# Later turns of the normalised input in the feed-forward stage of a transformer block, one core

## What is computed

```
x  = x + attention(layernorm(x))            # its last product, with Wo, is done in the last stage
h  = layer_norm(layernorm(x), ln1_g, ln1_b)
h  = gelu(h @ ternary(w1).T + b1)
h  = layer_norm(h, ln2_g, ln2_b)
x  = x + h @ ternary(w2).T + b2
```

## Time and profile before

| | |
|---|---|
| median of 3 runs | 3494.17 us (3492.02 to 3497.58) |
| the profiled execution | 3496.95 us, its span 3495.2 us, granted clock 0.989 |
| PE busy over the span | 3416.4 us (98%) |
| DVE / ACT / POOL busy | 75% / 66% / 75% |
| last stage | from about 2956 us to the end |

### The profile page before, as it was taken

One profiled execution on the slowest core, in us unless ns is written; L12 is line 12 of the kernel. 1 busy time (PEld: TensorE's weight loads), 2 busy tenths in 40 slices (PEclk: granted clock), 3 DMA queues, 4 the chain that ended last, 5 costly groups with the idle time before them and its releaser, 6 DMA issues. The chain is left out here.

```text
span 3495.2 us, 71907 instructions
## 1 busy us (share of the span) xinstructions
PE 3416.4 (98%) x21410; PEld 2203.3 (63%) x21410; DVE 2627.8 (75%) x4493; ACT 2297.5 (66%) x4412; POOL 2605.8 (75%) x1279
## 2 busy tenths in 40 slices
PE   6999999999999999999999999999999998999999
PEld 4655555555555555555555555666666654888888
DVE  6777777777777767777777777777777776899998
ACT  2766666776667667766667667776666665555555
POOL 2888888888888888888888888888888884222221
PEclk7999999999999999999999999999999998999999
DMA  5233322233333322333333323333322223333332
GB/s 195 83 95 105 107 95 99 94 122 101 101 101 122 101 83 99 118 101 101 101 118 100 101 96 119 101 101 101 119 92 92 74 84 103 94 98 92 98 99 67
DMA packets 255090, 355.75 MB, mean 102 GB/s; under 512 B 40221, under 2 KB 163485, under 8 KB 250269
## 3 DMA queue, kind: packets, MB, share of 16 engines
q1 hardware_dynamic: 245532, 343.29, 30.3%
q10 hardware_dynamic: 9216, 8.39, 0.7%
HBM read 219.49 MB, written 62.12 MB: 81 GB/s over the span
## 5 line engine op out<-in xcount | busy, mean ns | idle before, releaser
L463 POOL TENSOR_TENSOR prob_sum<-prob_sum,prob 128x1024 f32<-128x1024 f32 x762 | 1861.6, 2443 | 369.0 <-ACT prob L542 318.1
L542 ACT ACTIVATE prob<-scores 128x512 f32<-128x512 f32 x2048 | 1073.3, 600 | 524.2 <-PE scores L828 512.2
L752 DVE TENSOR_REDUCE row_max<-max_scores 128x1 f32<-128x512 f32 x1536 | 988.1, 684 | 435.0 <-PE max_scores L870 417.6
L1033 PE MATMUL attn_out<-prob,v 128*64 128x512 f32 x4096 | 934.9, 598 | 0.0
L819 PE MATMUL scores<-q_hi,k_hi 64*128 64x512 f32 x2048 | 786.7, 416 | 11.6 <-ACT prob L542 7.9
L824 PE MATMUL scores<-q_hi,k_lo 64*128 64x512 f32 x2048 | 755.7, 395 | 0.0
L828 PE MATMUL scores<-q_lo,k_hi 64*128 64x512 f32 x2048 | 752.1, 393 | 0.0
L1033 PEld LDWEIGHTS attn_out<-prob,v 128*64 128x64 f32 x4096 | 277.6, 137 | 566.6 <-issue 542.9
L870 PE MATMUL max_scores<-k_hi,q_hi 64*128 64x512 f32 x1536 | 579.2, 431 | 8.1 <-DVE row_max L752 5.0
L513 ACT ACTIVATE scores<-neg_max_seeds 128x512 f32<-128x512 f32 x1024 | 552.7, 599 | 48.8 <-DMA neg_max_seeds<-neg_max_halves 48.5
L819 PEld LDWEIGHTS scores<-q_hi,k_hi 64*128 64x128 f32 x2048 | 376.8, 185 | 290.1 <-issue 122.8
(11 more groups left out here) (148 smaller groups left out, 4771.6 us busy)
## 6 DMA issues: line engine op xcount, KB each, us to landing
rows<-rows SPq DMA_DIRECT2D x512, 128.0 KB, 2.0
neg_max_seeds<-neg_max_halves SPq DMA_DIRECT2D x128, 512.0 KB, 3.9
w_group<-w_parts SPq DMA_DIRECT2D x30, 1536.0 KB, 8.6
attn_normalised<-z_stage SPq DMA_DIRECT2D x128, 256.0 KB, 2.1
v<-attn_normalised SPq DMA_DIRECT2D x64, 512.0 KB, 4.1
sum_inverted_rows<-sums_inverted SPq DMA_DIRECT2D x126, 256.0 KB, 4.0
x_turned_parts<-x_tile_parts SPq DMA_DIRECT2D x49, 256.0 KB, 2.8
xt_batch<-x_turned_parts SPq DMA_DIRECT2D x7, 1792.0 KB, 9.3
```

The costliest lines, as they stand in the source:

```text
L463: nc.gpsimd.tensor_tensor(sums_of(k, half), a, prob[:, n % RING, :, :], ALU.add).then_inc(added, 1)
L542: nc.scalar.activation(prob[:, n % RING, e, :], S[e][n % 2][:, :], ACT.Exp).then_inc(exped[e], 1)
L752: nc.vector.reduce_max(mx[1 - u][:, e, n // 2, n % 2:n % 2 + 1], bank_of(e, jj)[:, :], axis=AX.X)\
L1033: nc.tensor.matmul(O[rows(e), :], V[k // 2 % 2][:, j, col:col + DH], prob[:, n % RING, e, :], start=j == 0, stop=j == 7).then_inc(pv_made[ ...
```

## The change

Three blocks of the last stage move inside the step functions; no instruction is added or dropped, and no wait condition is changed. On PE the two transposes `turn_b` go from between UP and `turn_c` to the end of the step, behind the down product. On ACT `h_turned_hi` goes from ahead of `g_turned_hi` to behind the gelu. On DVE `h_turned_lo` goes from the end of the step that turned the tile into the next step, between the gained gelu and `result`; it is thereby put under the phase UP.

```diff
@@ scalar
-                if at(j, q, Y_MADE):
-                    t, r = at(j, q, Y_MADE)
-                    wait(act, b_turned, t + 1)
-                    wait(act, up_made, 2 * t)
-                    nc.scalar.activation(hthi[:, :], TB[:, 0:KT * P], ACT.Copy).then_inc(ht_hi, 1)
                 if at(j, q, GATE):
...
                     nc.scalar.activation(gel[r % 2][:, :], up[:, :], ACT.Gelu, accum_out=gsum[r % 2][:, :]).then_inc(gelu_made, 1)
+                if at(j, q, Y_MADE):
+                    t, r = at(j, q, Y_MADE)
+                    wait(act, b_turned, t + 1)
+                    wait(act, up_made, 2 * t)
+                    nc.scalar.activation(hthi[:, :], TB[:, 0:KT * P], ACT.Copy).then_inc(ht_hi, 1)
                 if at(j, q, RES):
@@ vector
                                                    ALU.add, ALU.mult).then_inc(gained, 1)
+                if at(j, q, UP):
+                    t, r = at(j, q, UP)
+                    wait(dve, ht_hi, t + 1)
+                    wait(dve, up_made, 2 * t)
+                    nc.vector.tensor_tensor(htlo[:, :], TB[:, 0:KT * P], hthi[:, :], ALU.subtract).then_inc(ht_lo, 1)
                 if at(j, q, RES):
...
-                if at(j, q, Y_MADE):
-                    t, r = at(j, q, Y_MADE)
-                    wait(dve, ht_hi, t + 1)
-                    wait(dve, up_made, 2 * t)
-                    nc.vector.tensor_tensor(htlo[:, :], TB[:, 0:KT * P], hthi[:, :], ALU.subtract).then_inc(ht_lo, 1)
             steps(step)(dve)
@@ tensor
                         last.then_inc(up_made, 1)
-                if at(j, q, Y_MADE):
-                    t, r = at(j, q, Y_MADE)
-                    wait(pe, xg_made, t + 1)
-                    wait(pe, ht_lo, t)
-                    for k in range(KT):
-                        last = nc.tensor.transpose(TB[:, k * P:(k + 1) * P], xg[:, k * P:(k + 1) * P], ident[:, :])
-                    last.then_inc(b_turned, 1)
                 if at(j, q, GATE):
...
                     last.then_inc(down_made, 1)
+                if at(j, q, Y_MADE):
+                    t, r = at(j, q, Y_MADE)
+                    wait(pe, xg_made, t + 1)
+                    wait(pe, ht_lo, t)
+                    for k in range(KT):
+                        last = nc.tensor.transpose(TB[:, k * P:(k + 1) * P], xg[:, k * P:(k + 1) * P], ident[:, :])
+                    last.then_inc(b_turned, 1)
             steps(step)(pe)
```

## The result

| | before | after |
|---|---|---|
| median of 4 runs each | 3493.72 us | 3469.35 us (3466.45 to 3472.96) |
| ratio, 95% interval | | 0.9928 (0.9915 to 0.9940) |
| the profiled execution, its span | 3496.95, 3495.2 us | 3466.45, 3464.6 us |
| a step in the loop, mean of 56 | 8.164 us | 7.743 us |

What follows compares the result with a forecast made beforehand. A round over PE and DVE, `turn_b` waiting for `x_gained`, was taken as the bound; 19.3 us from loop steps, 0.5 from written-out steps and 0.3 from fill and drain gave 20.1 us, so 3474.1 us, range 3466 to 3485.

Steps and rivals of the forecast that it cites:

- What bounds, and why it goes: Loop of the last stage: a closed round over PE and DVE, `turn_b` waiting for `x_gained`, sets the 8.17 us step.
- PE's step: PE in the loop: 8.16 - 0.62 + 0.28 = 7.82 us per step, bounds 7.74 and 7.90.
- The removed part: PE between UP and `turn_c`: 2.48 us falls to 1.86, so 0.62 us go from a loop step.
- The part put in: `turn_b` behind the down product: 0.20 us from start to start, plus 0.08 on the first eight matmuls of Y.
- The gelu round: Negated mean, `h_turned_lo`, `up_biased`, gelu, next negated mean: 7.77 us, 0.05 under PE's step, bounds 7.69 and 7.91.
- DVE's list: DVE's same instructions, one of them moved, need 7.66 us per step, less than PE's 7.82.
- The rival in which this round takes over: Loop: the gelu round binds at 7.91 to 8.0 us per step, gain 9 to 14 us, 3480 to 3485; 22%.
- The delay at a turn of the loop: Register work a loop turn adds to DVE and ACT, hidden behind PE before, comes to light; part of the 22% rival.
- ACT's walk: ACT after Y's start: `h_turned_hi` from 0.3 us, `zn_hi` from 1.0 to 1.2, DVE's `zn_lo` about 2.1; no cost to PE.
- DVE alone: Loop: PE's step falls under DVE's, gelu round binds at 7.69 to 7.77 us; gain 23 to 27.5 us, 3467 to 3471; 15%.
- Fill and drain: Ends of the last stage: drain +1.7 us, fill about -2.0, together -0.3, bounds -2.5 and +1.7.
- the wait named: Drain, step 66: UP waits for `h_turned_lo` behind the gained gelu, +1.7 us.

Runs made afterwards that it cites:

- turn_constant: Kernel before, in its old order, but `turn_b` turns a constant tile (the bias rows) and PE does not wait for `x_gained`: 3462.55 us, one run.
- low_part_twice: Changed kernel, but DVE makes the low part of `turn_b` twice, first into a tile nobody reads: 3484.68 us.

## Why the prediction was right, and where it was off

The forecast was 3474.1, the measured 3469.35, within the range 3466 to 3485; faster, as forecast.

**What bounds, and why it goes: right.** `turn_constant` shows it without any move: take the wait away and the step is 7.74. The view that gave this was the chain, closed over PE and DVE; the waits view alone would have promised 0.19 or 0.63 per step, by the row that one takes, where 0.41 came.

**PE's step, 7.82 forecast, 7.75 measured: a term mis-sized.** The removed part was right: UP to `turn_c` is 1.87 after, 1.86 in the earlier trace rows. The part put in was 0.20 + 0.08; measured is 0.14 + 0.08 = 0.22 behind the down product, and 0.22 again in the old place without its wait. The row for the 0.20 was from a step in which `turn_b` had itself waited for `x_gained`, so its weight load lay bare; where nothing is awaited that load starts ahead, beside the down product. The weight loads of the two, in the fill of before and in the loop after (the transposes start at 2972.24 and at 3347.08):

```profile
2972.24 0.20 PEld L1307 LDWEIGHTS turn_b<-ident,x_gained 128*128 128x128 f32 x2 [0.39 <-DVE x_gained L1258]
...
3346.98 0.24 PEld L1325 LDWEIGHTS turn_b<-ident,x_gained 128*128 128x128 f32 x2
```

The old step's 0.27 to `turn_c` carried the same excess. This is 0.06 of the 0.07 per step, and most of the 4 us between the loop's forecast 19.3 and its 23.6.

**The gelu round, 7.77 forecast, 7.58 measured: too high by three small things.** The terms of the recorded sum add up to 7.78. `h_turned_lo` has a pitch of 0.33, not 0.41; the step from `up_biased` to the gelu costs 0.03, not 0.12 (1.43 from start to start); and the negated mean follows by 1.18. Durations of neighbours overlap by 0.06 to 0.1, and I had used them where pitches were to be had. The same goes for DVE's list: 7.66 forecast, 7.53 measured. The conclusion "0.05 under PE's" was thereby too near: it is 0.17. The rival in which this round takes over, given 22%, was further off than I thought, and `low_part_twice` shows that it starts at about 0.17 us more for DVE. The delay at a turn of the loop, which I feared there, does appear: the first two steps of a turn take 7.86 and 8.0 by DVE's starts. That it is the register work, and not the branch, was assumed and not tested. DVE makes it good with steps of 7.58 behind them, and PE, with 1.1 us of cover, never sees it.

**ACT's walk: right**, to 0.1 us: `h_turned_hi` 0.36 behind Y (0.3), `zn_hi` 1.06 (1.0 to 1.2), `zn_lo` 2.15 (2.1). The strict order of ACT's queue that the Trainium skill states (TensorE: Matmul & The Clock Gate, Architectural detail) agrees with it: `zn_hi` does not pass `h_turned_hi`, which waits 0.43 us for `turn_b`.

**The case "DVE alone" did not occur**, though its band of times (3467 to 3471) holds the result. PE binds at 7.75: with 0.24 us less for PE the step falls, with DVE alone as the bound it could not. Y still takes 0.120 per matmul with nothing awaited. By the formula of that page of the Trainium skill (Back-to-back issue gap), which the page gives for isolated matmuls, it would be 0.109, and no run here shows that.

**Fill and drain.** The drain cost 1.9 (1.7 forecast), by the wait named. The fill gave 3.1 (2.0 forecast), in three parts. The first, 0.9, is the granted clock ahead of UP of step 3, which no term of the prediction held and the change did not cause. The second, 0.8, lies between that UP and the first gained gelu (4.72 us instead of 5.53): ahead of the first gelu ACT loads a table, 1.28 us, and that load stood behind the wait of `h_turned_hi`, where now it comes during it. This the prediction had left out. The third, 1.4, lies from there to step 6: `turn_c` no longer waits behind `turn_b` in step 4 and runs at the 2.4 GHz level, where before PE had sat idle for 2.48 us and then had a mean granted clock of 0.54 from 2979.91 to 2983.60. The rows of before stand ahead of those of after:

```profile
2973.12 1.28 ACT L1198 ACT_TABLE_LOAD   x1
...
2980.35 1.91 PE L1316 MATMUL turn_c<-ident,gelu_gained 128*128 128x128 f32 x8
...
2963.02 1.28 ACT L1193 ACT_TABLE_LOAD   x1
...
2972.71 1.03 PE L1309 MATMUL turn_c<-ident,gelu_gained 128*128 128x128 f32 x8
```

What the order and what the clock gave in this third part was not separated. PE's move alone (`pe_only`) gained 1.3 us in the fill: 0.5 by the clock in the first part, nothing in the second (5.54 us), 0.8 in the third. Without the clock's 0.9, fill and drain come to the -0.3 us of the forecast, though by parts that it had not all named.

## What to carry to other kernels

When two busy engines wait for each other in a ring, look for a small consumer that stands directly behind a short cover and could run a few microseconds later; here that cost nothing once its consumers had moved along on every engine. A part of the move is a gamble: PE's part alone gave 20 us, PE's and ACT's without DVE's cost 69 (`pe_and_act`: +2%). Price the insertion by a row in which the operation waited for nothing, and use starts, not durations, for rounds. An order with room (2 us for `x_gained`) has a shorter mean step than a tighter one with the same sum when an engine is delayed now and then, as at the turns of this loop: 7.743 against 7.798. The times could not show it, for the drain gave most of it back. Before a gain in a short stretch is credited to a change, look at the granted clock in it.

## What was not expected of the hardware

The wait of PE cost about twice what the idle mark of its matmuls shows, and less than that of its weight loads: 0.19 and 0.63 us marked, 0.41 gained. Two float32 transposes of 128 columns cost PE 0.22 us in all three places that were tried, behind matmuls of 512 columns, behind other transposes and behind matmuls of 256 columns, and the step came to 7.74 to 7.76 us in all four kernels without a regular wait. The same 50 matmuls and transposes at the start of the stage took PE 10.47 us in one kernel and 11.43 in another with the same order on PE, with a mean granted clock of 1.00 against 0.63 in their last 3.2 and 4.7 us.
